# The last stage of a Macaron block on one core in a new order, with its first tile's projection inside the scan's last units

## The reference, cut to what matters

```
x = x + 0.5 * ffn(layernorm(x))
x = x + ssm(layernorm(x))
x = x + 0.5 * ffn(layernorm(x))

ffn(x) = gelu(x @ W1b.T + b1) @ W2b.T + b2          # 256 -> 1024 -> 256, weights are signs times a row's mean
ssm, behind a norm, an input projection, a 4-tap convolution (xc) and projections to dt, B and C:
      h_t = h_(t-1) * dA_t + dt_t * B_t * xc_t      # 512 channels x 16 states
      every tenth step h is scaled down where its norm is over 20
      y_t = sum over states of h_t * C_t, plus D * xc_t
      ssm(x) = x + 0.5 * sigmoid(s) * ((y * silu(gate)) @ W_out.T)
```

## Time and profile before

| | us |
|---|---|
| median of 3 runs | 1732.75 |
| lowest and highest | 1728.92, 1733.2 |
| the profiled execution | 1729.7 |
| its span (first to last instruction) | 1727.9 |
| busy: PE, DVE, ACT, POOL | 1403.9, 1420.5, 1317.5, 975.1 |
| granted clock of TensorE, mean | 0.897 |

### The profile page before, as it was taken

One profiled execution on the slowest core, in us unless ns is written; L12 is line 12 of the kernel. 1 busy time (PEld: TensorE's weight loads), 2 busy tenths in 40 slices (PEclk: granted clock), 3 DMA queues, 4 the chain that ended last, 5 costly groups with the idle time before them and its releaser, 6 DMA issues.

```text
span 1727.9 us, 23094 instructions
## 1 busy us (share of the span) xinstructions
PE 1403.9 (81%) x6362; PEld 1080.8 (63%) x6362; DVE 1420.5 (82%) x1698; ACT 1317.5 (76%) x3384; POOL 975.1 (56%) x1318
## 2 busy tenths in 40 slices
PE   6999999996388778777777787777777777898987
PEld 5555555552276667666666677666666666676765
DVE  7666776565799999999999999999999999676773
ACT  5376666779899999999999999999999965223232
POOL 1301222220588888888888888888888887200000
PEclk9999999999678897989888888888988887899998
DMA  7223353333323333333333243343323337335430
GB/s 233 74 74 123 101 156 118 111 106 112 92 76 104 95 95 87 93 98 81 94 92 97 74 108 79 97 102 90 98 75 92 85 104 204 108 104 164 129 110 25
DMA packets 202688, 179.78 MB, mean 104 GB/s; under 512 B 82816, under 2 KB 175040, under 8 KB 202560
## 3 DMA queue, kind: packets, MB, share of 16 engines
q1 hardware_dynamic: 201616, 176.99, 36.3%
q10 hardware_dynamic: 944, 1.31, 0.2%
HBM read 125.26 MB, written 53.57 MB: 103 GB/s over the span
## 4 chain that ended last, share of the span: by engine, by line
PE 41%; ACT 29%; POOL 10%; DVE 9%; issue 9%; DMA 1%; ACTq 0%; POOLq 0%; SPq 0%; DVEq 0%
ACT tb L959 13%; PE banks L915 10%; ACT decay L987 7%; POOL hc L874 6%; PE banks L347 6%; PE banks L339 5%; ACT sc_sq L970 5%; PE banks L1238 4%; PE banks L1249 3%; PE banks L314 3%; DVE h L1076 3%; PE banks L1218 3%; DVE cv L612 3%; POOL rc L866 3%; PE banks L898 2%
## 5 line engine op out<-in xcount | busy, mean ns | idle before, releaser
L1076 DVE TENSOR_TENSOR_SCAN h<-decay,banks 128x704 f32<-128x704 f32 x410 | 661.1, 1612 | 27.1 <-ACT banks L995 23.7
L915 PE MATMUL banks<-hc,w_ident 128*128 128x160 f32 (+1 forms) x3296 | 662.5, 354 | 17.0 <-POOL hc L874 13.2
L915 PEld LDWEIGHTS banks<-hc,w_ident 128*128 128x128 f32 x3296 | 569.6, 227 | 39.5 <-POOL hc L874 29.2
L874 POOL TENSOR_TENSOR hc<-h,bc 128x640 f32<-128x640 f32 x410 | 589.7, 1439 | 0.0
L959 ACT ACTIVATE tb<-dtc,a 128x320 f32<-128x320 f32 (+1 forms) x832 | 449.5, 556 | 0.0
L898 PE MATMUL banks<-sc_ss,sc_ones 128*128 128x1 f32 x820 | 167.0, 273 | 244.9 <-ACT sc_sq L970 232.4
L1064 DVE TENSOR_TENSOR banks<-banks,bc 128x640 f32<-128x640 f32 x410 | 341.3, 833 | 30.1 <-DVE h L1076 0.9
L898 PEld LDWEIGHTS banks<-sc_ss,sc_ones 128*128 128x128 f32 x820 | 145.2, 220 | 330.0 <-ACT sc_sq L970 327.7
L987 ACT ACTIVATE decay<-tb 128x640 f32<-128x640 f32 x410 | 298.3, 728 | 0.4
L866 POOL TENSOR_TENSOR rc<-qs,w_mhalf 128x1 f32<-128x1 f32 x410 | 224.8, 548 | 61.5 <-POOL qs L861 1.3
L257 POOL TENSOR_TENSOR ln_rz<-ln_vz,w_mhalf 128x4 f32<-128x4 f32 x8 | 13.9, 1734 | 281.2 <-DVE ln_vz L585 281.2
(11 more groups left out here) (110 smaller groups left out, 1629.6 us busy)
## 6 DMA issues: line engine op xcount, KB each, us to landing
bc<-scratch_blk SPq DMA_DIRECT2D x205, 320.0 KB, 3.4
uc<-scratch_u SPq DMA_DIRECT2D x35, 240.0 KB, 4.3
scratch_xc<-xc SPq DMA_DIRECT2D x8, 1024.0 KB, 4.8
scratch_sg<-sg SPq DMA_DIRECT2D x8, 1024.0 KB, 5.9
scratch_dt<-dt SPq DMA_DIRECT2D x8, 1024.0 KB, 5.6
scratch_u<-u SPq DMA_DIRECT2D x8, 1024.0 KB, 6.6
q_ys<-scratch_y SPq DMA_DIRECT2D x8, 1024.0 KB, 6.6
q_xc<-scratch_xc SPq DMA_DIRECT2D x8, 1024.0 KB, 8.9
```

Of the source, the lines that this page charges most:

```text
L874: pool.tensor_tensor(hc[:, pl % 2, :, j % 2 * S:(j % 2 + 1) * S] .rearrange("p (c b n) e -> p c b n e", c=KE, b=B)[:, :, b], state(m)[:, : ...
L915: mm = pe.matmul(psY[:, 0:KE * B * wide], w.ident[:], rhs, start=(n == 0), stop=(n == N - 1))
L1076: dve.tensor_tensor_scan(state(m).rearrange("p r e -> p (r e)"), decay[:, m % DRING], psI[m % B][:, 0:NCH * W], 0.0, ALU.mult, ALU.add).th ...
```

## The change

It has four parts, shown in the diff.

1. `scan_stage`: the last block's u is no longer moved to PSUM, VectorE reads it from `uc` in SBUF. That frees psX's banks earlier, and `project` of tile 0, cut in pieces of 2 matmuls, stands in units 404 to 409, with its last 4 matmuls behind the last unit. The four gates of tile 0 go from units 400, 402, 404 and 406 to units 399 to 402.
2. `tensor` of the last stage: up's first group stands in the tile before; the projection of the next tile stands behind up's group 3; down's two halves are apart, with the transposes of xn between them; the transposes of y stand behind the next tile's first up group. Down waits for each group of g by itself. The last tile turns y in two halves.
3. `vector`: the residual stands behind split 3, `apply` behind split 4, then splits 5 to 7, `skip` of tile i + 2, `low_x` of tile i + 1, `gate` of tile i + 2, and the final add last. The last tile's final add is done in two halves, each stored on its own. ScalarE copies xn's high part between the two scalings of y.
4. `sync`: the stores of tile i - 1 stand behind the fetches of tile i + 2.

```diff
--- before.py
+++ after.py
@@ scan_stage, tensor
-            if m % (HB * B) == 4 and m // (HB * B) + 1 < HALVES:
+            if m % (HB * B) == 4 and m // (HB * B) + 1 < HALVES - 1:
                 move_u(m // (HB * B) + 1)
             p, quarter = (m - 4) // 4, m % 4
             if p >= 0:
                 readout(p, quarter * 4, quarter * 4 + 4)
+
+            if m >= UNITS - 6:
+                q, k = (m - UNITS + 6) // 2, (m - UNITS + 6) % 2 * (KE // 2)
+                pe.wait_ge(inp_ready, (HALVES - 2 + q // 2) * HB * B)
+                post.project(pe, 0, q, k, k + KE // 2)
+        post.project(pe, 0, G - 1, 0, KE)
         for p in range((UNITS - 4) // 4, PAIRS):
-            n0 = (UNITS % 4) * 4 if p == (UNITS - 4) // 4 else 0
-            if n0:
-                pe.wait_ge(inp_ready, UNITS)
-                post.project(pe, 0)
-            readout(p, n0, N)
+            readout(p, (UNITS % 4) * 4 if p == (UNITS - 4) // 4 else 0, N)
@@ scan_stage, vector
+            if g == HALVES - 1:
+                u = uc[g % 2][:].rearrange("p (c b) t -> p b c t", b=B)
...
-            if k in (10, 8, 6, 4):
-                post.gate(dve, 0, (10 - k) // 2)
+            if k in (11, 10, 9, 8):
+                post.gate(dve, 0, 11 - k)
@@ post_stage, sync
         def store(i):
-            sp.wait_ge(res_ready, i + 1)
             for b in range(B):
+                sp.wait_ge(res_ready, i + 1 + (b if i == LAST else 0))
...
-            store(i)
+            if i >= 1:
+                store(i - 1)
+        store(TILES - 1)
@@ post_stage, tensor
+        def down(i, d, k0, k1):
+            if i >= 1:
+                pe.wait_ge(yT_ready, KD * (i - 1) + d + 1)
+            for k in range(k0, k1):
+                pe.wait_ge(split_lo, KH * i + k + 1)
+                for half in range(2):
+                    mm = pe.matmul(psD[:, d, :], w.s2[:, k, d * P:(d + 1) * P], g[:, half, k, :],
+                                   start=(k == 0 and half == 0), stop=(k == KH - 1 and half == 1))
+            if k1 == KH:
                 mm.then_inc(dn_done, 1)
...
         turn_xn(0)
         pe.wait_ge(scan.y_copied, PAIRS)
+        up(0, 0, 1)
         for i in range(TILES):
-            up(i)
-            if i + 1 < TILES:
-                project(pe, i + 1)
-            down(i)
-            if i + 1 < TILES:
+            up(i, 1, KH // 2)
+            if i < LAST:
+                for q in range(G):
+                    project(pe, i + 1, q, 0, KE)
+            up(i, KH // 2, KH)
+            down(i, 0, 0, KH)
+            if i < LAST:
                 turn_xn(i + 1)
-            turn_y(i)
+                down(i, 1, 0, KH)
+                up(i + 1, 0, 1)
+                turn_y(i)
+        down(LAST, 1, 0, KH // 2)
+        pe.wait_ge(x2_ready, TILES)
+        turn_last(0)
+        down(LAST, 1, KH // 2, KH)
+        turn_last(1)
@@ post_stage, scalar
         for i in range(TILES):
             gelus(i)
-            scale_y(i)
+            scale_y(i, 0)
             if i + 1 < TILES:
                 high_x(i + 1)
+            scale_y(i, 1)
@@ post_stage, vector
         for i in range(TILES):
-            low_x(i)
-            split_g(i)
-            if i + 2 < TILES:
-                product(i + 2)
+            split_g(i, 0, KH // 2)
             if i + 1 < TILES:
                 residual(i + 1)
+            split_g(i, KH // 2, KH // 2 + 1)
+            if i + 1 < TILES:
                 apply(i + 1)
-            finish(i)
+            split_g(i, KH // 2 + 1, KH)
+            if i + 2 < TILES:
+                for k in range(KE):
+                    skip(dve, i + 2, k)
+            if i + 1 < TILES:
+                low_x(i + 1)
+            if i + 2 < TILES:
+                for k in range(KE):
+                    gate(dve, i + 2, k)
+            if i < LAST:
+                finish(i)
+        finish_last()
```

More of the change, by code:

```diff
@@ L1208, in gpsimd, with project @@
             rstd(i)
-    def project(pe, i):
-        pe.wait_ge(gated, KE * (i + 1))
-        if i == 0:
-            pe.wait_ge(w_in, 16)
-        if i >= 2:
-            pe.wait_ge(res_ready, i - 1)
-        for q in range(G):
-            for k in range(KE):
-                mm = pe.matmul(psX[:, q, :], ys[i % 2][:, k, q * P:(q + 1) * P], wout[:, k, :],
-                               start=(k == 0), stop=(k == KE - 1))
-        mm.then_inc(proj_done, 1)
+    def project(pe, i, q, k0, k1):
+        if q == 0 and k0 == 0:
+            if i == 0:
+                pe.wait_ge(w_in, 16)
+            if i >= 2:
+                pe.wait_ge(res_ready, i - 1)
+        pe.wait_ge(gated, KE * i + k1)
+        for k in range(k0, k1):
+            mm = pe.matmul(psX[:, q, :], ys[i % 2][:, k, q * P:(q + 1) * P], wout[:, k, :],
+                           start=(k == 0), stop=(k == KE - 1))
+        if q == G - 1 and k1 == KE:
+            mm.then_inc(proj_done, 1)
     def tensor(pe):
@@ L1228, in turn_xn, with up @@
                 mm.then_inc(t1_done, 1)
-        def up(i):
+        def up(i, m0, m1):
             pe.wait_ge(hi_ready, KD * (i + 1))
             pe.wait_ge(lo_ready, KD * (i + 1))
-            for m in range(KH):
+            for m in range(m0, m1):
                 if i * KH + m >= 2:
@@ L1240, in up @@
                 mm.then_inc(up_done, 1)
-        def down(i):
-            pe.wait_ge(split_lo, KH * (i + 1))
+        def down(i, d, k0, k1):
             if i >= 1:
-                pe.wait_ge(yT_ready, KD * i)
-            for d in range(KD):
-                for k in range(KH):
-                    for half in range(2):
-                        mm = pe.matmul(psD[:, d, :], w.s2[:, k, d * P:(d + 1) * P], g[:, half, k, :],
-                                       start=(k == 0 and half == 0), stop=(k == KH - 1 and half == 1))
+                pe.wait_ge(yT_ready, KD * (i - 1) + d + 1)
+            for k in range(k0, k1):
+                pe.wait_ge(split_lo, KH * i + k + 1)
[3 more added lines that the diff above has]
+            if k1 == KH:
                 mm.then_inc(dn_done, 1)
@@ L1254, in turn_y @@
             pe.wait_ge(yT_ready, KD * (i + 1))
-            if i + 1 < TILES:
-                pe.wait_ge(x2_ready, i + 2)
+            pe.wait_ge(x2_ready, i + 2)
             for q in range(G):
@@ L1353, in low_x, with split_g @@
                                   ALU.subtract).then_inc(lo_ready, 1)
-        def split_g(i):
-            if i >= 1:
+        def split_g(i, m0, m1):
+            if i >= 1 and m0 == 0:
                 dve.wait_ge(dn_done, KD * i)
-            for m in range(KH):
+            for m in range(m0, m1):
                 dve.wait_ge(gelu_done, i * KH + m + 1)
@@ L1369, in finish, with finish_last @@
             dve.tensor_tensor(res[:, i % 2], psX[:], x2[:, i % 2], ALU.add).then_inc(res_ready, 1)
-        def product(i):
-            for k in range(KE):
-                skip(dve, i, k)
-            for k in range(KE):
-                gate(dve, i, k)
+        def finish_last():
+            dve.wait_ge(stored[LAST % 2], 32 * (LAST // 2))
+            for n in range(2):
+                dve.wait_ge(t2_done, TILES + n)
+                half = slice(2 * n, 2 * n + 2)
+                dve.tensor_tensor(res[:, LAST % 2, half], psX[:, half], x2[:, LAST % 2, half], ALU.add
+                                  ).then_inc(res_ready, 1)
         residual(0)
+        for k in range(KE // 2):
+            skip(dve, 1, k)
         apply(0)
-        product(1)
+        for k in range(KE // 2, KE):
+            skip(dve, 1, k)
+        low_x(0)
+        for k in range(KE):
+            gate(dve, 1, k)
         for i in range(TILES):
-            low_x(i)
-            split_g(i)
-            if i + 2 < TILES:
-                product(i + 2)
+            split_g(i, 0, KH // 2)
             if i + 1 < TILES:
                 residual(i + 1)
+            split_g(i, KH // 2, KH // 2 + 1)
+            if i + 1 < TILES:
                 apply(i + 1)
-            finish(i)
+            split_g(i, KH // 2 + 1, KH)
[5 more added lines that the diff above has]
+            if i + 2 < TILES:
+                for k in range(KE):
+                    gate(dve, i + 2, k)
+            if i < LAST:
+                finish(i)
+        finish_last()
     return Post(sync, gpsimd, tensor, scalar, vector, load_params, fetch, project, residual_scale, residual_steps,
```

27 lines of the change are left out of this document (17 added, 10 removed).

## The result

| | before | changed |
|---|---|---|
| median of 5 runs each, us | 1728.92 (1722.98 to 1733.2) | 1708.9 (1705.82 to 1720.02) |
| ratio, with its 95% interval | | 0.9888 (0.9853 to 0.9924) |
| the profiled execution, us | 1729.7, span 1727.9 | 1720.02, span 1718.2 |

The change makes the kernel 1.1% faster, 19.4 us by the ratio. The profiled execution of the changed kernel is the slowest of its five. The same kernel was run again beside the experiments: median 1707.28, ratio 0.9871 (0.9836 to 0.9907), profiled at 1709.54.

The account below looks back on a forecast made before the run. The last stage was taken as TensorE-bound with one 2.56 us hole a tile. Start -13.8, six periods -10.4, end -3.5, clock +3.5: -24.2 from 1729.7 gives 1705.5, forecast as 1706 us; range 1698 to 1718.

Parts of the forecast that it names:

- The steady tile: Last stage, projection to projection in the new order: 26.15 us at full clock instead of 27.02.
- the hole: TensorE's 2.56 us gap a tile before up: 2.1 comes back as three short waits on VectorE's splits.
- rival 1: Last stage: the short waits don't come back, TensorE runs back to back in every tile; 1687 us, 5%.
- The clock: Last stage: half-busy waits slow TensorE's clock, 7 x 0.26 x 1.95 = 3.5 us charged; bounds nothing and 18.
- -10.4: Last stage, six tile periods: 156.9 us against 167.3 before, without the clock's cost.
- Rival 2: Last stage: the clock falls at the short waits in every tile, 18 us instead of 3.5; 1720 us, 10%.
- Rival 4: Last stage: the clock drops and stays at half through the dense 16 us behind the waits; 1737 us, 4%.
- The start: Scan's end to tile 0's up: first residual 4.6 us earlier, up 7.8 earlier, tile 0's projection end 13.8 earlier.
- 0.7 us charged for the pieces: Scan's last units: delay from tile 0's projection matmuls, two a unit, with TensorE's unit about equal to VectorE's.
- Rival 3: Scan's last six units: the projection pieces meet the half clock, costing 5 to 13 us; 1711 to 1718 us, 12%.
- u from SBUF: Scan's last block: VectorE's product of 640 elements takes 0.8 us as from PSUM, within 0.2 either way.
- The end: Last projection to the kernel's end: 37.05 us against 40.6 before, a gain of 3.5.

Follow-up runs that it names:

- pad_in: The changed kernel with two unread VectorE products a tile added between the normalising and split 5; one run, 1725.63 us.
- pad_out: The changed kernel with two unread VectorE products a tile added between split 3 and the residual; one run, 1705.09 us.
- one_wait: The changed kernel, but TensorE waits once for all eight splits ahead of down's first half; one run, 1744.04 us.
- fill: The changed kernel with five spare matmuls a tile in the places of TensorE's short waits; median 1704.98 us, ratio 0.9856 to before.
- post_only: Only the new last stage, over the old end of the scan with tile 0's projection whole; median 1712.2 us, ratio 0.9901 to before.
- whole_end: The changed kernel with the last tile's y turned whole behind all of down, one final add and both stores behind it; one run, 1711.02 us.
- scan_only: Only the scan's changes (projection pieces, gates' new units, u from SBUF), over the old last stage; median 1726.23 us, ratio 0.998 to before.
- split_last: The changed kernel with the projection behind up's group 7 of 8, the last group and its split beside the norm; median 1692.23 us, ratio 0.9778 to before.

## Why the prediction was right, and where it was off

The forecast was 1706 us, with -24.2 from the profiled time of 1729.7; measured were -19.4 and about -22.

- **The steady tile** is the walk of the prediction, almost row by row. From the end of the projection: residual at 0.02 (0.20 predicted), down's first half done at 9.96 (9.95), transposes to 10.83 (10.8), down's second half to 14.48 (14.45), group 0 to 15.38 (15.4), transposes of y to 16.44 (16.5). Only then it parts: up's groups 1 to 3 take 3.00 instead of 2.75, and the period at the full clock is 26.4 instead of 26.15. That the hole doesn't go but comes back as three short waits (against rival 1) is shown by the waits' rows, by pad_in and pad_out; they are 0.93, 0.33 and 0.33 us long instead of 1.2, 0.45 and 0.45, and the last pair behind one takes 0.74 instead of 0.62, so that two small errors partly cancel. Six times 0.25 is 1.5 us of the miss. The prediction called itself wrong if the period was over 28 us. The mean period is 27.2, but each of the three with a fall is 28.04 to 28.08, just beyond that bound, which left the prediction's own clock term out.
- **The clock** was the mis-sized term. The step "26% of the time at the low level, times 1.95" gave 3.5 us over seven tiles. Measured: three of six periods at 1.66, which is 5.0, and 1.3 more at up 0, where I had counted no fall (12.44 to the next residual; 11.1 in the kernels that had none there). 6.3 instead of 3.5. Neither factor of the term held: the scan's share of 0.26 says nothing of waits that recur with a tile, half of the tiles were hit; and one hit costs 1.66. Before's own six periods hold 4.9 us of falls too (167.0 less six times 27.02), all of which the -10.4 had taken as won and the 3.5 had given back in part. So in these periods the falls cost as much after the change as before, and what the new order won there, 3.6, is six times 0.6 at the full clock.
- **Rival 2**, every tile, is what `one_wait` shows: there it took longer waits than the new order has. Here the page that I weighed (the Trainium skill, "TensorE: Matmul & The Clock Gate", section "A second HAM failure mode: psum-queue depth-cycling") was nearer in kind than my 26%: its case, short idles between groups of matmuls and a clock that swings between its two levels, is what the trace shows, with 0.54 in the window at 1553, and `fill`, in which TensorE waits 0.27 us a tile instead of 1.6, has no fall. It has no rate, though, and "every tile", my reading of it, is not what came.
- **Rival 4**, slow through the dense work behind the waits: no; by 1560 the groups are at 0.91 again.
- **The start**: residual 0 at -4.6 and -6.7 (-4.6 predicted), up 0 at -7.7 and -9.9 (-7.8). Of it 5.4 + 3.15 = 8.6 is the change, against 5.3 (without the delay) and 3.2 of the prediction; the rest is the scan ahead of it, so that the exact hit of the first execution is in part luck. The first residual is at 1496.33 by the clock of the execution, beyond the 1490 that I had set as a bound for being wrong. That bound was badly put: the execution was 10.0 us late at unit 392 already, and the distance from there is as forecast. In the second execution the first residual is at 1485.82. The 0.7 us charged for the pieces can't be told: to the last scan it is +0.9 and -1.3 in the two executions of the same kernel, and post_only, without pieces, has -1.5.
- **Rival 3**, pieces at half clock for 5 to 13 us: one piece met it, 1.53 us instead of 1.03 and 1.25 us of waiting in one scan; in the second execution two scans wait 1.18 us each. Not more.
- **u from SBUF**: 0.83 us as predicted.
- **The end** was -3.6, -3.5 predicted, and that is in part luck. I gave 0.45 to the store and about 0.5 to the halved add; `whole_end` has neither and ends 0.3 us later only. And 2.2 of the 3.6 is the fall of the clock in the last up of before, which `scan_only`, with the old order, doesn't have (8.32 us there):

```profile
1699.13 10.89 PE L1238 MATMUL banks<-q_xT,w_s 128*128 128x512 f32 x32 [2.56 <-issue]
```

That leaves 1.4 us, 38.31 less 36.95, for the order of the last tile, the halves included. Why the new order has no such fall there, I have not tested.

So 1.5 and 2.8 us of the miss of 4.8 are named. In the second comparison the miss is about 2 us only, since the start came out 2.1 us better than forecast, of which 1.3 lies ahead of the last unit's scan.

## What to carry to other kernels

When a wait is taken away by reordering, walk the ring that the new order makes, from the late producer through each engine's queue and back: here it came out to 0.25 us, and it also showed where to put work for nothing (ahead of the residual) and what would take the ring off TensorE. A dependence that crosses to another engine and back is hidden by work that is ready when it starts, not by work that waits in the same engine's queue behind it; the changed kernel had 32 matmuls there, but the last six of them wait for splits that stand behind the norm on VectorE, and with 28 that wait for one split only (`split_last`) the period went from 26.4 to 24.1. A wait of TensorE costs its own length and, some of the time, the clock behind it, so many short waits are to be priced with the fall, and spare matmuls in them can pay for themselves (by the periods 5 us in `fill`; its time alone doesn't show it). And the falls of the kernel before are to be counted on both sides: a gain read against a tile that had a fall is partly the clock's.

## What the runs showed of the hardware

- GpSimd's power on 128x4 elements took 1.01 us with VectorE idle (before), 1.11 beside VectorE's splits, 1.39 beside its gates and 1.46 beside its skips. The same instruction differs by up to 0.45 us with what VectorE does at the time. The Trainium skill, "SBUF — State Buffer", section "SBUF: two separate sides", has a VectorE instruction with two SBUF inputs and a GpSimd one that reads SBUF take a shared pair of ports as an exclusive lock. The gates and skips have two SBUF inputs, as the splits' low parts have; the direction agrees with these rows. The rule doesn't say why gates and skips should cost more than splits, and no run here tests the lock alone.
- Falls of the clock recur on the same tiles in four executions, every second tile, in periods of 28.04 to 28.08 us. I had taken them for random.
- Transposes of 128x128 took 1.71 us for eight at half clock and 0.87 at the full one; the loss of one fall was 1.64 to 1.66 us in the steady tiles of the new order, 1.35 right behind up 0 and 1.6 to 2.2 in three tiles of `one_wait`, by a half of down alone.
- Executions of unchanged code differ by some microseconds: 19 runs of before lie between 1717.87 and 1739.9 us. That is more than each single step of this change, and it is why the steps were read from distances inside the trace.
